# A fused attention and expert layer in 16 chunks: small transposes moved from TensorE to VectorE in 32x32 blocks

## The reference

```python
xn  = layernorm(x)                                   # no scale, no shift
qkv = xn @ w_qkv + b_qkv                             # 16 heads of 16 dimensions
# heads 0-3: causal attention; heads 4-15: causal attention over the last 64 positions
att = softmax(q k^T / 4, masked) @ v  ->  @ w_out + b_out
Q, K = xn @ W_Q.T, xn @ W_K.T
invQ, invK = Q @ W_inv.T, K @ W_inv.T
def branch(q, k, V, W, U, b):                        # 8 experts of rank 64
    prod = (q V) * cumsum(k W over the sequence)
    wts  = softmax(gelu(q @ r1.T + b1) @ r2.T + b2 + expert_bias)
    return (sum over experts of wts * prod @ U + wts @ b) / position
ffn = (branch(Q, K, fwd) + alpha * branch(invQ, invK, inv)) @ W_O.T
out = x + att + ffn
```

## Time and profile before

| what | value |
|---|---|
| time, 3 runs | median 1515.61 us (1514.74 to 1518.65) |
| profiled execution | 1516.97 us, of which the span of its instructions is 1515.3 us |
| granted TensorE clock, mean | 0.996 of full speed |
| busy: TensorE, VectorE, ScalarE, GpSimd | 1425.3, 882.5, 852.4, 575.5 us |
| DMA | 150.56 MB, mean 99 GB/s |

### The profile page before, as it was taken

The page is one execution under the profiler, slowest core; times in us unless marked ns, Lnnn a source line. Parts: engine busy times, 40 slices in busy tenths (PEclk is TensorE's granted clock), DMA queues, the critical chain, the costliest instruction groups (busy, mean ns, idle before and its releaser), DMA issues.

```text
span 1515.3 us, 36826 instructions
## 1 busy us (share of the span) xinstructions
PE 1425.3 (94%) x14977; PEld 1072.4 (71%) x14977; DVE 882.5 (58%) x1935; ACT 852.4 (56%) x1512; POOL 575.5 (38%) x663
## 2 busy tenths in 40 slices
PE   5999999999999999999999999999999999999997
PEld 4577775867758686686857777586775868678673
DVE  6676773556645675465755577356664567546451
ACT  3446557474665547565474645647466563756544
POOL 1044351444425343352424435143442524335241
PEclk9999999999999999999999999999999999999999
DMA  9322507253251625317053350615325162531600
GB/s 226 81 77 75 145 23 170 65 121 118 64 144 32 156 82 120 102 39 187 31 141 96 83 144 30 162 60 121 118 73 136 32 165 73 120 102 40 174 30 15
DMA packets 153789, 150.56 MB, mean 99 GB/s; under 512 B 28468, under 2 KB 136885, under 8 KB 153573
## 3 DMA queue, kind: packets, MB, share of 16 engines
q1 hardware_dynamic: 153620, 148.22, 37.7%
HBM read 106.98 MB, written 34.87 MB: 94 GB/s over the span
## 4 chain that ended last, share of the span: by engine, by line
PE 75%; DVE 11%; ACT 8%; issue 5%; POOL 1%; DMA 0%; ACTq 0%; POOLq 0%; DVEq 0%
PE PS L660 35%; PE PS L781 11%; PE PS L815 3%; PE PS L932 3%; PE PS L801 3%; PE PS L901 3%; PE PS L869 3%; PE PS L883 3%; ACT HE L1116 2%; PE PS L913 2%; PE PS L987 2%; PE PS L845 2%; ACT HE L1108 2%; DVE block_peak L1292 2%; DVE PL L1384 1%
## 5 line engine op out<-in xcount | busy, mean ns | idle before, releaser
L1547 POOL TENSOR_TENSOR PL<-prod,PH 128x512 fp32r<-128x512 f32 x128 | 164.7, 1287 | 215.1 <-ACT PH L1078 215.1
L1542 POOL TENSOR_TENSOR prod<-prod,rest 128x512 f32<-128x512 f32 x96 | 123.3, 1287 | 265.1 <-ACT prod L1068 146.0
L660 PE MATMUL PS<-XH,WH 128*128 128x512 f32 x512 | 218.3, 426 | 4.5 <-DVE XL L1232 1.9
L1292 DVE TENSOR_REDUCE block_peak<-PS 128x4 f32<-128x512 f32 x288 | 181.0, 684 | 54.2 <-PE PS L815 54.2
L660 PE MATMUL PS<-XL,WH 128*128 128x512 f32 x512 | 203.7, 398 | 0.0
L660 PE MATMUL PS<-XH,WL 128*128 128x512 f32 x512 | 203.2, 397 | 0.0
L1078 ACT ACTIVATE PH<-prod 128x512 fp32r<-128x512 f32 x128 | 80.8, 631 | 209.6 <-DVE prod L1365 209.5
L1525 POOL TENSOR_SCALAR_AFFINE_SELECT HE<-HE 128x256 f32<-128x256 f32 x128 | 51.0, 411 | 347.9 <-ACT HE L1116 345.3
L1116 ACT ACTIVATE HE<-PS 128x512 f32<-128x512 f32 (+1 forms) x320 | 159.7, 552 | 24.8 <-PE PS L883 22.6
L1068 ACT ACTIVATE prod<-PS 128x512 f32<-128x512 f32 x128 | 76.1, 594 | 125.3 <-PE PS L660 114.9
L1285 DVE TENSOR_REDUCE peak<-PS 128x4 f32<-128x512 f32 x192 | 120.6, 682 | 41.1 <-PE PS L801 41.1
(11 more groups left out here) (196 smaller groups left out, 3142.3 us busy)
## 6 DMA issues: line engine op xcount, KB each, us to landing
parts_d<-area SPq DMA_DIRECT2D x32, 768.0 KB, 5.1
area<-parts_d SPq DMA_DIRECT2D x128, 192.0 KB, 8.4
rest<-weights_d SPq DMA_DIRECT2D x192, 128.0 KB, 2.9
area<-parts_d SPq DMA_DIRECT2D x32, 576.0 KB, 8.4
tok<-in_L_attn_x_dram SPq DMA_DIRECT2D x16, 512.0 KB, 6.3
xt<-in_L_attn_x_dram SPq DMA_DIRECT2D x16, 512.0 KB, 4.2
wide<-weights_d SPq DMA_DIRECT2D x64, 128.0 KB, 3.0
out_dram<-xt SPq DMA_DIRECT2D x16, 512.0 KB, 3.7
```

The costliest lines, as they stand in the source:

```text
L660: ins = e.matmul(ps, a, b, start=first and k == 0, stop=last and k == n - 1, skip_group_check=True)
L1292: e.tensor_reduce(block_peak[ch % NC][:, t, :, j], psum(i).rearrange("p (a k) -> p a k", a=4), AX_X, ALU.max).then_inc(bank_read[i])
L1542: e.tensor_tensor(prod[:, j % 3, :], prod[:, j % 3, :], wide[j % WIDE], ALU.mult).then_inc(weighed)
L1547: e.tensor_tensor(PL[:, j % 2, :], prod[:, j % 3, :], PH[:, j % 2, :].bitcast(F32), ALU.subtract).then_inc(plo)
```

## The change

- TensorE makes none of the small transposes any more: L728, L737, L826, L913 and L922 go, and with them the ScalarE copies L1043, L1056, L1102 and L1125.
- Context: VectorE turns each group straight from its PSUM bank in 32x32 blocks (`ctx`), divides there, and turns two groups together back (`cturn`, k = 0 in the local phase, k = 1 in the tail). ScalarE takes the high part from SBUF; the low part is subtracted by GpSimd (`crest`). The rows of w_out are loaded in the order that fits (16 small loads for one).
- `finish` is cut in two: the first half (k = 0) stands after the last global product, the second (k = 1) in the next chunk, behind its first peak matmuls.
- Local groups use banks 7, 4, 7 in turn where all used bank 7.
- Logits: 8 matmuls of 256 columns; VectorE turns them from PSUM. The three bf16 parts of the weights are turned by VectorE in the same transpose as the weights, cast by ScalarE, and put into `WT` by SyncE through DRAM: four writes, a wait for them, three reads, and `open` waits for the reads.
- Peaks: VectorE turns them before it splits them; SyncE writes four small DMAs where it wrote one.

```diff
+                elif kind == "ctx":
+                    e.transpose(craw[:, 1, :], psum(cb)).then_inc(bank_read[cb])
...
+                    q.step(e.reciprocal(cinv[:, :], raw_t[:, :, HD]))
+                    q.wait_step()
+                    q.step(e.tensor_tensor(ctok[:, k, :].rearrange("p (b e) -> p b e", e=32)[:, :, half * HD:(half + 1) * HD], raw_t[:, :, 0:HD],
+                                           cinv[:, :].unsqueeze(2).to_broadcast([P, C // 32, HD]), ALU.mult))
...
+                elif kind == "cturn":
+                    e.transpose(cturned, ctok[:, k, :]).then_inc(ctx_turned)
...
+                elif kind == "crest":
+                    q.wait_ge(ctx_hi, nth(*stage))
+                    e.tensor_tensor(PL[:, k, :], cturned, PH[:, k, :].bitcast(F32), ALU.subtract).then_inc(ctx_lo)
...
                 elif kind == "open":
-                    q.wait_ge(bank_read[7], use("bank7", "weight_rows", ch))
+                    q.wait_ge(rows_in, 16 * 3 * (ch + 1))
...
+                elif kind == "weight_rows":
+                    q.wait_ge(rows_cast, ch + 1)
+                    q.wait_ge(rows_in, 16 * 3 * ch)
+                    for w in range(2):
+                        for h in range(2):
+                            row = 32 * (2 * w + h)
+                            e.dma_start(rows_d[:, KE * w:KE * (w + 1), h * HALF:(h + 1) * HALF], weights_b[row:row + 3 * KE, :]).then_inc(rows_out, 16)
+                    q.wait_ge(rows_out, 16 * 4 * (ch + 1))
+                    q.wait_ge(opened, ch)
+                    for n, lo, hi in ((0, 0, 3), (1, 3, 5), (2, 5, 6)):
+                        e.dma_start(WT[2 * KE * lo:2 * KE * hi, :], rows_d[n:n + 1].to_broadcast([hi - lo, 2 * KE, C])).then_inc(rows_in, 16)
...
         run(experts[0] + peaks[0])
+        if ch:
+            add_finish(ch - 1, 1)
...
         weave(local_groups(ch), side)
         add_lav(ch, NL // 4, 1)
+        add("cturn", ch, 0)
         if nxt:
             add("keep", ch + 1)
             add("stacks", ch + 1, "local")
...
+        add("crest", ch, 0)
...
+        side.append([(add_finish, ch, 0)])
         weave(order, side)
         if nxt:
             add("stacks", ch + 1, "global")
             add("weight_rows", ch + 1)
-        add_cout(ch, 0)
         if nxt:
             add_weigh(ch + 1, 0)
             run([(add_x, ch + 1, 1, part) for part in range(2)])
             add_weigh(ch + 1, 1)
-        for k in range(DB):
-            add_on("cparts", ch, k, uses=[score_use()])
+        add("cturn", ch, 1)
         if nxt:
             run([(add_x, ch + 1, 2, part) for part in range(2)])
             add_weigh(ch + 1, 2)
-        add_finish(ch)
+        add("crest", ch, 1)
+    add_finish(CHUNKS - 1, 1)
```

## The result

The changed kernel takes 1662.97 us (median of 4 runs, 1659.25 to 1667.9) against 1515.43 us: a ratio of 1.0971, 95% interval 1.0933 to 1.1009. It is slower, as forecast, but by 147 us where I had 38: the time lies far outside my range.

| piece | forecast | measured |
|---|---|---|
| prologue, to the first open (82.31, now 100.28) | +13 | +18.0 |
| eight opens that end a c = 0 chunk | +40.8 | +80.0 (12.1 the first, 67.8 the seven others) |
| seven opens that end a c = 1 chunk | -12.3 | +41.5 |
| from the last open to the end | -3 | +2.7 |
| sum | +38.5 | +142.2 |

The account below looks back on a forecast made before the run. TensorE bounds most of the kernel, but its savings meet late queues: +13 prologue, +40.8 c = 0 opens, -12.3 c = 1 chunks, -3 rest make +38.5, 1555.5 profiled, median 1554 us; own range 1536 to 1578, with rivals 1506 to 1588.

Parts of the forecast that it names:

- seven opens that end a c = 1 chunk: Between opens, each c = 1 chunk gains 0.5 + 0.2 + 0.9 + 0.15 = 1.75 us; seven times, -12.3.
- from the last open to the end: Last chunk and rest: context path about 2 us shorter, early `finish` waits some 2, earlier phases gain; -3 us.
- The step that failed: Local phase: `hidden` becomes limited by VectorE instead of TensorE, so only 0.2 of 2.6 us is kept per chunk.
- The open after a c = 0 chunk: `WT` through DRAM comes 5.4 us late; less 0.3 gained, 5.1 us lost, eight times: +40.8.
- the sign that I named: If the forecast is right, TensorE idles 3 us at every second open, waiting for SyncE's reads of the weights' rows.
- The tail of a c = 1 chunk: Transposes go, but `finish` k = 1 newly waits 1.4 us for `crest`; net gain 0.15 us.
- the open behind it: Open after a c = 1 chunk: `WT` arrives in time, no wait, with a cover of 0.4 to 1.4 us.
- PSUM transposes: Local phase: VectorE's turn of 512 elements from PSUM taken as 0.7 us, bounds 0.4 to 1.24.
- Prologue: Before the first open: `WT` is there at 95.4 where the open was at 82.31; +13 us (+10 to +16).
- TensorE's busy time: Whole kernel: a sign of being right was TensorE's busy time down by 85 to 90 us while the span grows.
- The rival that TensorE's time is simply saved: `WT` arrives before TensorE reaches the open and VectorE catches up: -88, prologue +10, 1438 us (half: 1480); chance 0.17.
- my fourth case: VectorE becomes the bound: PSUM transposes at 1.24 us and waits for GpSimd, 1578 to 1590 us; chance 0.08.

Follow-up runs that it names:

- e1: Changed kernel with the context's first turn back, and so ScalarE's copy, placed behind the next chunk's four hidden stages: 1609.7 us, ratio 1.0624.
- e7: Changed kernel with the six matmuls of hidden 1 carried out three times instead of once in 15 chunks: 1638.81 us, ratio 1.0805.
- e2: Changed kernel with the norm's last piece behind the second turn back and `crest` k = 1 ahead of GpSimd's third gate product: 1680.69 us, ratio 1.1086.
- e11: Changed kernel with the low parts of the turned context subtracted by VectorE instead of GpSimd, order unchanged: 1677.88 us, ratio 1.1081.
- e10: Changed kernel with gelus first, tail reordered, `WT` rows written early, VectorE subtracting low parts, first open later, `found` behind the last gate product: 1485.97 us, ratio 0.9801.

## Why the prediction was wrong

**The step that failed** is in the local phase: "So `hidden` moves from a TensorE limit to a VectorE limit, and I keep 0.2 us of 2.6." I followed the banks that `hidden` needs back to VectorE's q parts. VectorE's L1196, the L1256 of before, was indeed what hidden 0 and 1 waited for, 0.29 and 0.18 us. But I never followed the banks that hidden 2 and 3 need, which the gelus of 0 and 1 free, through ScalarE's queue, where the new copy stands ahead of them. Forecast: 0.2 us gained per chunk. Measured: 4.3 us of idle time and 1.5 of slow matmuls lost, 15 times, 87 us. e1 shows that it is the copy's place and e7 that the slow matmuls are the clock's. It is most of the miss in the c = 1 chunks, not all: without it (e1) they are at +9.4 us in place of +41.5, where I had -12.3. In the c = 0 chunks taking it away gains 8 us only, since the open still waits for `WT`.

**A term that was missing everywhere: the clock.** Every wait of mine was priced at its own length. One of 4.3 us costs 5.8; one in front of an open after a c = 0 chunk puts a slow stretch at the head of the c = 1 chunk, which is what made e2 and e11 slower.

**The open after a c = 0 chunk**: the mechanism was right, several sizes were off. The write's issue is 3.04 us for four, not 1.2: I priced it by a write of a plainer shape. By the steps of my sum, start to start: from the first write to the last 2.36 us (I had 0.9), from there to the first read 1.92 (1.7), to the last read 1.77 (0.6), to the open 3.59 (2.9). From the first write to the open that is 9.6 us in place of 6.1; in 12 of the 14 places where the open waits it is 8.2 to 8.3, with 2.5 for the last step. On the other side I let `crest` go by GpSimd's backlog alone and left out that VectorE's norm stands ahead of the turn back: a wait of 3.27 us and its slow stretch. The two lie partly on top of each other, as I had said of 5.1: TensorE reached the open later too, so that the sign that I named, 3 us idle in front of every second open, came out at 1.5 us on average.

By the Trainium skill (DMA: Bandwidth & Descriptors, "Latency and other measured facts") a DMA has a fixed cost of about 2 us. From the start of the last issue the write took 1.92 us, near that figure, and the last read 2.5 in most places and 3.59 in the tail above, more than it.

**The tail of a c = 1 chunk**: a wait of 1.4 us for `crest` forecast, 1.35 to 1.38 measured. But the open behind it, which I had covered by 0.4 to 1.4 us, waited 0.6 to 0.9 us in five of seven places: 8.2 us from write to open are 2.1 more than my 6.1. The x block waits for ScalarE's copy, 10.3 us in 15 places. **PSUM transposes**: 0.7 us taken between bounds of 0.4 and 1.24, 0.710 measured. **Prologue**: +13 forecast (to +16), +18.0 measured: the first gate product ended at 90.9 us in place of 88.1, and from the first write to the open it took 8.2 us in place of 6.1. The first of these varies from execution to execution: in e1, e11 and e7, whose prologue is the same, the product ended at 86.6, 88.0 and 92.5, and the prologue came out at +13.6, +15.1 and +19.5. So 2.1 us of the miss are mine and the rest isn't shown to be. **TensorE's busy time**: I said 85 to 90 us less. It was unchanged: the transposes were worth 50 (e10), and the lower clock took as much.

**The rival that TensorE's time is simply saved** fell at 1438, but its mechanism is what e10 brings out in part: 30 us. It was overpriced. I counted 0.75 us per context group, 0.64 of it busy time, while matmuls overlap and the next stage starts sooner: by start to start a group's four take 0.40, and L922, 1.03 us long, held the order up for 0.85. All five kinds take 4.1 us in a chunk of before, not 5.5, with 0.9 of waits ahead of them in a c = 0 chunk and 1.3 in a c = 1 chunk. e10 is faster by 3.3 us in the middle one of its c = 1 chunks (2.3 to 3.5) and by 2.5 in that of its c = 0 chunks, the first left out (0.9 to 2.7). Where the rest went chunk by chunk was not tried.

The Trainium skill (SBUF — State Buffer, "Who interferes with whom") has VectorE and GpSimd exclude each other in some modes. In the tail above VectorE's L1323 takes 1.32 us beside a gate product of GpSimd, and 0.42 in the local phase with none; of the norm's four L1165 the first, beside the same product, takes 1.27 and the others 0.40 each. Over the whole trace, the 24 L1323 with no GpSimd operation beside them take 0.42 to 0.43 us, the 40 with one 0.57 to 1.53. The trace agrees, and these two delays, 1.8 us, are part of the 3.27. VectorE as the bound, my fourth case, didn't come: in e10 it is busy for 1017 us, 40 more than in the change, and the kernel is 177 us faster.

## What to carry to other kernels

When work is moved to another engine, walk each engine's queue in order, also those that gain only one small copy, and ask what stands *behind* the new instruction, not only what it waits for. Price an idle stretch of TensorE of a few us at its length and the slow matmuls behind it; an edit that only moves a stop to a place on the critical path can lose. Judge single edits by the view of waits as much as by the time: of three delays in a row, taking one away shows a fraction of its worth, or less than nothing, until the next is gone too.

## What the runs showed of the hardware

A stop of 4.30 us was followed by a granted clock of 0.50 (1.2 GHz) in 15 places of 15, a stop of 1.49 us at the same place in none (e7): filling the wait with 2.9 us of useless matmuls made the kernel 24 us faster. A short stop isn't always free: of the seven of 1.35 to 1.38 us in the c = 1 tails of the change, two were followed by it. The Trainium skill (TensorE: Matmul & The Clock Gate, "Part 1: The HAM clock gate") says that the lower level is the default and activity releases it. The windows above agree: in both stops the clock falls while TensorE stands still, and it comes back while TensorE works.

VectorE's transposes from PSUM in 32x32 blocks take 449 ns for 256 columns and 710 for 512, so 1.02 ns for each further column. The Trainium skill (Vector Engine (DVE) Microarchitecture Reference, 3.8 "The reshape front-end and per-opcode configuration") has this transpose sustain one element per cycle and lane. The even growth with the columns agrees (311, 445 and 709 ns for 128, 256 and 512 columns from SBUF); how long a cycle is, no run here shows.

Issuing a small DMA costs SyncE's queue time that goes by its shape more than by its bytes. A write of the weights holds it for 0.59 us in the kernel before, in runs of 128 bytes, and for 0.30 in the changed one, in runs of 1 KB, both 8 KB; a write of the bf16 rows, 12 KB in runs of 512 bytes, for 0.70 (medians of 64 each). Four of these are the 3.04 us that others wait behind.
